# Sorting 800 tokens by group of experts in the last stage of a fused decoder kernel

## The reference, cut to what matters

```
x = rmsnorm(src + self_attention(src), norm1_w)        # 800 tokens x 256
shared = swiglu(x @ W_shared_in) @ W_shared_out        # 256 -> 2*512 -> 512 -> 256
g_probs = softmax(x @ Wg_gate + group_bias)            # 2 groups
g_idx = argmax(g_probs)
e_probs = softmax(x @ We_gate + expert_bias, over the 4 experts of group g_idx)
w = the two largest of e_probs * g_probs[g_idx], zero for the other 6 experts
h = swiglu(x @ W1_shared)                              # one hidden row for all experts
routed = sum over e of (h @ W2_experts[e]) * w[:, e]   # 8 experts, 512 -> 256
out = rmsnorm(x + shared + routed, norm2_w)
result = x_layer + tanh(g_ffn[1]) * out
```

## Time and profile before

| what | us |
|---|---|
| median of three runs | 582.63 (580.09 to 582.83) |
| the profiled execution, its own time | 584.23 |
| its span | 582.4 |
| TensorE busy in the span | 532.8 (91%) |
| VectorE, ScalarE, GpSimd busy | 282.0, 183.7, 125.6 |

### The profile page before, as it was taken

The page is one execution under the profiler, slowest core; times in us unless marked ns, Lnnn a source line. Parts: engine busy times, 40 slices in busy tenths (PEclk is TensorE's granted clock), DMA queues, the critical chain, the costliest instruction groups (busy, mean ns, idle before and its releaser), DMA issues. The chain is left out here.

```text
span 582.4 us, 9223 instructions
## 1 busy us (share of the span) xinstructions
PE 532.8 (91%) x3429; PEld 345.9 (59%) x3429; DVE 282.0 (48%) x660; ACT 183.7 (32%) x438; POOL 125.6 (22%) x146
## 2 busy tenths in 40 slices
PE   0989899899999879999999899999889999999995
PEld 0736575355556567788877677878535544544442
DVE  3436553121235575665676968887625222224242
ACT  1134331211103344555555545656532110000000
POOL 3112005001117252232232635341000000000000
PEclk9999968999999988999999999999989999999998
DMA  7989942279976697595573056000012000000000
GB/s 211 237 227 322 392 181 58 74 273 378 400 250 202 165 257 186 138 236 166 134 183 81 2 190 246 2 2 1 1 52 62 1 1 0 1 0 29 0 19 9
DMA packets 47087, 78.15 MB, mean 134 GB/s; under 512 B 6867, under 2 KB 36543, under 8 KB 46941
## 3 DMA queue, kind: packets, MB, share of 16 engines
q1 hardware_dynamic: 43841, 68.32, 38.0%
q0 software_dynamic: 3200, 9.22, 4.9%
HBM read 63.97 MB, written 12.13 MB: 131 GB/s over the span
## 5 line engine op out<-in xcount | busy, mean ns | idle before, releaser
L1392 PE MATMUL pb<-ring,big 128*128 128x512 f32 (+2 forms) x320 | 108.7, 593 | 2.3 <-DVE big L1343 1.2
L1392 PE MATMUL pb<-split 128*100 128x362 f32 (+2 forms) x320 | 78.3, 329 | 6.7 <-DVE nmx L1184 2.7
L1392 PEld LDWEIGHTS pb<-ring,big 128*128 128x128 f32 (+2 forms) x320 | 44.1, 166 | 59.4 <-issue 54.9
L1184 DVE TENSOR_REDUCE nmx<-pb 100x1 f32<-100x361 f32 x128 | 62.7, 527 | 25.6 <-PE pb L1392 25.2
L1392 PEld LDWEIGHTS pb<-split 128*100 128x100 f32 (+2 forms) x320 | 55.9, 183 | 16.7 <-issue 6.1
L860 ACT ACTIVATE big<-pb 121x400 f32<-121x400 f32 (+1 forms) x96 | 48.2, 505 | 23.9 <-PE pb L1392 21.6
L1364 DVE SCALAR_TENSOR_TENSOR ctxbuf<-pb,ctxbuf 128x256 f32<-128x256 f32 x48 | 23.2, 484 | 55.5 <-PE pb L1392 54.6
L1392 PE MATMUL pb<-big,arena 121*32 121x100 f32 (+3 forms) x1072 | 47.9, 264 | 1.5 <-ACT arena L710 1.2
L1392 PE MATMUL pb<-hT,ring 128*128 128x400 f32 x128 | 43.8, 501 | 0.5 <-DVE big L1343 0.5
L637 POOL TENSOR_TENSOR shift<-consts,nmx 100x400 fp32r<-100x400 f32 x32 | 28.3, 884 | 64.6 <-DVE nmx L1184 64.5
L1392 PE MATMUL pb<-hT,wgu 128*128 128x400 f32 (+2 forms) x108 | 39.7, 516 | 0.9 <-ACT hT L919 0.6
(11 more groups left out here) (242 smaller groups left out, 784.7 us busy)
## 6 DMA issues: line engine op xcount, KB each, us to landing
ring<-in_L_ffn_gate_up_proj SPq DMA_DIRECT2D x12, 1024.0 KB, 9.6
split<-kx_dram SPq DMA_DIRECT2D x64, 181.0 KB, 3.8
ring<-in_L_ffn_down_proj SPq DMA_DIRECT2D x12, 512.0 KB, 7.3
kx_dram<-split POOLq DMA_DIRECT2D x16, 362.0 KB, 4.9
ctxbuf<-in_L_ffn_gate_up_proj SPq DMA_DIRECT2D x4, 1024.0 KB, 9.6
ring<-in_L_ffn_W_experts SPq DMA_DIRECT2D x4, 1024.0 KB, 11.4
split<-qx_dram SPq DMA_DIRECT2D x64, 50.0 KB, 2.0
ctxbuf<-in_ctxT SPq DMA_DIRECT2D x6, 361.0 KB
```

The lines of the kernel that those rows point to most:

```text
L1184: nc.vector.tensor_reduce(nmx[:, t % 4, q:q + 1], PB[SB[n % 3]][0:T, 0:CTX], AX.X, ALU.max, negate=True) \
L1392: return nc.tensor.matmul(o, l, r, start=start, stop=stop)
```

## The change

Tokens are sorted by group into 928 slots: group 0 from slot 0 up, group 1 from slot 927 down, with 128 unused slots between. A tile is 116 slots, so no tile holds tokens of both groups, and each of the 8 tiles needs the down products of four experts alone. Which four is known only at run time: TensorE reads an offset for each tile into a register and addresses w2 with it.

- Logits are computed by batch, tokens on partitions. A product with a lower triangle and seven with ones give each token its position (as in layer 0), VectorE turns it into a slot.
- GpSimd scatters rows, token number and logits (267 numbers a row) of each batch to memory, then one scatter of 128 rows of zeros into the unused slots; SyncE loads them back by tiles, two tiles to a load of 116 partitions. Gates, transposes and the W1 units work on the sorted rows.
- Shared units and shared down products stay in token order. x + shared is added up by batch (e_base) and scattered to eb_dram, the rows of x to ex_dram; both get zeros in the unused slots first. Both come back by parts of two tiles (load_base, load_rest), some of them behind final products (e_down).
- The first half's shared units (0 to 3) stand among the last output products of attention; the first four batches are scaled (rms_rows) inside the attention loop, into free places of arena (stage).
- The result is stored by an indirect DMA of GpSimd for each tile, by token number; unused slots carry a number that is out of bounds.
- ScalarE takes exponentials of the gates between the silus of the shared and of the W1 units.

The diff, cut to its core:

```diff
-STARTS = [0, 128, 256, 768, 384, 512, 640]
-NF = len(STARTS)
-TAIL = STARTS.index(NT // 128 * 128)
-TAILN = NT % 128
-WHOLE = [c for c in range(NF) if c != TAIL]
-PARTS = [(0, 4), (4, 6), (6, 7)]
+ET = 116
+NS = NX * ET
+EX = D + 1 + 2 + NX
+FPARTS = [(0, 3), (3, 6), (6, 7), (7, 8)]
...
+            sp.wait_ge(s("b_scat"), 16 * (2 * NB + 1))
+            for g in range(NX // 2):
+                sp.dma_start(sorted_rows[0:ET, 2 * g:2 * g + 2, :],
+                             es_dram[2 * ET * g:2 * ET * (g + 1), :].rearrange("(i p) d -> p i d", p=ET)).then_inc(s(f"b_xg{g}"), 16)
+            sp.wait_ge(s("e_bst"), 16 * (NB + 1))
+            sp.wait_ge(s("n_tp"), NB // 2 * (turn("e") + 1) + NX // 2)
+            sp.wait_ge(s("e_gx"), 1)
+            def load_base(g):
+                sp.dma_start(hF[0:ET, 2 * g:2 * g + 2], eb_dram[2 * ET * g:2 * ET * (g + 1), :].rearrange("(i p) d -> p i d", p=ET)) \
+                    .then_inc(s(f"ld_F{g}"), 16)
+            def load_rest(g):
+                sp.dma_start(xF[0:ET, 2 * g:2 * g + 2], ex_dram[2 * ET * g:2 * ET * (g + 1), :].rearrange("(i p) d -> p i d", p=ET)) \
+                    .then_inc(s("ld_x"), 16)
+            load_base(0)
+            load_base(1)
+            sp.wait_ge(s("e_xst"), 16 * (NB + 1))
+            load_rest(0)
+            for g in range(1, NX // 2):
+                sp.wait_ge(s("e_down"), NB + 2 * g - 1)
+                load_rest(g)
+                if g >= 2:
+                    load_base(g)
+            sp.wait_ge(s("stored"), 16 * NX)
...
+            pool.wait_ge(s("n_hN"), NB * (turn("e") + 1))
+            pool.wait_ge(s("b_xs"), NB + 1)
+            pool.wait_ge(s("b_slot"), 3)
+            for b in range(NB):
+                nc.gpsimd.indirect_dma_start(es_dram, bass.IndirectOffsetOnAxis(slot[:, b:b + 1], 0), stage(b), None,
+                                             bounds_check=NS - 1, oob_is_err=False).then_inc(s("b_scat"), 16)
+            nc.gpsimd.indirect_dma_start(es_dram, bass.IndirectOffsetOnAxis(spare[:, 0:1], 0), zero_rows[:], None,
+                                         bounds_check=NS - 1, oob_is_err=False).then_inc(s("b_scat"), 16)
+            for d, name in ((eb_dram, "e_bst"), (ex_dram, "e_xst")):
+                nc.gpsimd.indirect_dma_start(d, bass.IndirectOffsetOnAxis(spare[:, 0:1], 0), zero_rows[:, 0:D], None,
+                                             bounds_check=NS - 1, oob_is_err=False).then_inc(s(name), 16)
+            for b in range(NB):
+                pool.wait_ge(s("e_base"), b + 1)
+                nc.gpsimd.indirect_dma_start(eb_dram, bass.IndirectOffsetOnAxis(slot[:, b:b + 1], 0), hN[:, b, :], None,
+                                             bounds_check=NS - 1, oob_is_err=False).then_inc(s("e_bst"), 16)
+            pool.wait_ge(s("c_res"), NB)
+            for b in range(NB):
+                nc.gpsimd.indirect_dma_start(ex_dram, bass.IndirectOffsetOnAxis(slot[:, b:b + 1], 0), x[:, b, :], None,
+                                             bounds_check=NS - 1, oob_is_err=False).then_inc(s("e_xst"), 16)
+            pool.wait_ge(s("b_tok"), 2)
+            for part, (a, z) in enumerate(FPARTS):
+                inverse_root("f", stdF, rstdF, only=part)
+                for i in range(a, z):
+                    pool.wait_ge(s("f_out"), i + 1)
+                    nc.gpsimd.indirect_dma_start(flat_out, bass.IndirectOffsetOnAxis(tok[0:ET, i:i + 1], 0), xF[0:ET, i, :], None,
+                                                 bounds_check=NT - 1, oob_is_err=False).then_inc(s("stored"), 16)
...
+            d_turned_copy(NB - 2)
+            d_sums_copy(NB - 1)
+            e_turned(0)
+            e_turned(1)
+            square(NB - 3)
+            shared_silu(0)
+            d_turned_copy(NB - 1)
+            square(NB - 2)
+            shared_silu(1)
+            square(NB - 1)
+            shared_silu(2)
+            e_turned(2)
+            shared_silu(3)
+            e_turned(3)
+            for u in range(4, 2 * FT):
+                shared_silu(u)
+            for g in range(NX // 2):
+                act.wait_ge(s("n_tp"), NB // 2 * (turn("e") + 1) + g + 1)
+                nc.scalar.activation(hTs[:, :, 2 * ET * g:2 * ET * (g + 1)], bank3(4 + g % 2, KT, 2 * ET), ACT.Copy) \
+                    .then_inc(s("n_hT"), 1)
+            act.wait_ge(s("e_gx"), 1)
+            nc.scalar.activation(ge, gl, ACT.Exp).then_inc(s("e_gexp"), 1)
...
+                if n == 28:
+                    rms_variance(0)
+                if n in (29, 30):
+                    rms_rows(0, range(2 * (n - 29), 2 * (n - 28)))
...
             rms_variance(1)
             rms_rows(1)
+            shared_hidden(0)
+            d_residual(NB - 1)
+            rms_variance(2)
+            shared_hidden(1)
+            rms_rows(2)
             link(nc.vector.tensor_scalar(growF, brow["n2"][:], tg[:, 3:4], None, ALU.mult))
+            shared_hidden(2)
+            shared_hidden(3)
...
+                dve.wait_ge(s(f"ld_F{i // 2}"), 16)
+                for p in range(2):
+                    v = 2 * i + p
+                    dve.wait_ge(s("e_down"), NB + v + 1)
+                    link(nc.vector.scalar_tensor_tensor(out=hF[0:ET, i, :], in0=PB[v % 8][0:ET, 0:D], scalar=we[:, i, 2 * p:2 * p + 1],
+                                                        in1=hF[0:ET, i, :], op0=ALU.mult, op1=ALU.add))
+                    nc.vector.scalar_tensor_tensor(out=hF[0:ET, i, :], in0=PB[v % 8][0:ET, D:2 * D], scalar=we[:, i, 2 * p + 1:2 * p + 2],
+                                                   in1=hF[0:ET, i, :], op0=ALU.mult, op1=ALU.add).then_inc(s("e_comb"), 1)
...
+            def shared_unit(u):
+                half, f = u // FT, u % FT
+                if u >= 2:
+                    pe.wait_ge(s("e_hid"), u - 1)
+                if u % FT == 0:
+                    pe.wait_ge(s("n_hT"), NB // 2 * turn("e") + 2 * (half + 1))
+                for w in range(2):
+                    for k in range(KT):
+                        last = mm(PB[S_BANKS[u % 2][w]][:, 0:HALF], wgu2[:, 0, k, F * w + 128 * f:F * w + 128 * f + 128],
+                                  hT[:, k, HALF * half:HALF * (half + 1)], k == 0, k == KT - 1)
+                last.then_inc(s("e_gu"), 1)
+            pe.wait_ge(s("d_max"), NG * NB)
+            ln_pe("e", range(0, 2), stage, E_TURN)
             d_to_tokens(NB - 1)
+            pe.wait_ge(s("ld_we"), 16 * 6)
+            pe.wait_ge(s("d_ptsb"), NG * NB)
+            shared_unit(0)
             bank6_part("Y", NB - 2, 0)
             d_turn_back(NB - 1)
+            shared_unit(1)
             bank6_part("Y", NB - 1, 0)
...
+            shared_unit(2)
+            ln_pe("e", range(2, 3), stage, E_TURN)
+            shared_unit(3)
+            pe.wait_ge(s("d_x2"), NB)
+            ln_pe("e", range(3, 4), stage, E_TURN)
+            for b in range(NB):
...
+                pe.wait_ge(s("n_hT"), NB // 2 * turn("e") + b // 2 + 1)
                 for k in range(KT):
...
+                    last = mm(PB[4][0:T, (2 + NX) * b:(2 + NX) * (b + 1)], hT[:, k, T * b:T * b + T], wge[:, k, :],
                               k == 0, k == KT - 1)
...
+            last.then_inc(s("lg"), 1)
+            shared_unit(4)
+            pe.wait_ge(s("b_oh"), 2)
+            mm(PB[5][0:T, 0:NB], consts[0:T, cs["lower"]], nflag, True, False)
+            for d in range(1, NB):
+                mm(PB[5][0:T, d:NB], ones[0:T, 0:T], nflag[:, 0:NB - d], False, d == NB - 1)
+            mm(PB[5][:, NB:NB + 1], ones[0:T, 0:128], nsum, True, True).then_inc(s("b_pos"), 1)
+            for u in range(5, 2 * FT):
+                shared_unit(u)
+            pe.wait_ge(s("b_slot"), 4)
+            for b in range(NB):
+                pe.wait_ge(s("e_hid"), FT if b < NB // 2 else 2 * FT)
+                for f in range(FT):
+                    last = mm(PB[shared_bank(b)][0:T, 0:D], hidS[:, f, T * b:T * b + T], wdn[:, f, :], f == 0, f == FT - 1)
+                last.then_inc(s("e_down"), 1)
...
+                pe.wait_ge(s(f"b_xg{g}"), 32)
+                if g < 2:
+                    pe.wait_ge(s("e_base"), g + 1)
+                else:
+                    pe.wait_ge(s("n_hT"), NB // 2 * (turn("e") + 1) + g - 1)
+                for k in range(KT):
+                    for q in range(2):
+                        at = (2 * k + q) * ET
+                        last = nc.tensor.transpose(PB[4 + g % 2][:, at:at + ET], sorted_rows[0:ET, 2 * g + q, 128 * k:128 * k + 128],
+                                                   ident[0:ET, 0:ET])
+                last.then_inc(s("n_tp"), 1)
...
+            for u in range(2 * FT, 4 * FT):
+                half, f = u // FT - 2, u % FT
+                if f == 0:
+                    pe.wait_ge(s("n_hT"), NB // 2 * (turn("e") + 1) + 2 * (half + 1))
+                if u < 2 * FT + 3:
+                    pe.wait_ge(s("e_base"), NB)
+                else:
```

(51 more changed lines are left out.)

240 lines of the change are left out of this document (87 added, 153 removed).

## The result

The changed kernel took 563.32 us, the median of four runs (558.8 to 565.35), beside 582.73 us (580.09 to 584.34) for the kernel before, measured beside it. The ratio is 0.9652 with a 95% interval of 0.9607 to 0.9696. That is 19.4 us less, where 24.3 were forecast (558.3 us, range 552.5 to 566.9). The profiled execution took 563.71 us, with a span of 561.8.

What follows compares the result with a forecast made beforehand. TensorE's matmul stream, busy 91% of the span, was taken as the bound. The stream ends 25.5 us earlier (32.0 - 6.5), the end is 1.2 longer: 24.3 us less, span 558.1, forecast 558.3 us, range 552.5 to 566.9.

Steps and rivals of the forecast that it cites:

- the clock: Rival, chance 0.20: thin logits and position products lower TensorE's clock for ten to fourteen us, giving 561.4 to 563.4 us.
- the units: Rival, chance 0.07: shared units don't fit beside attention's last batches, each waits behind ScalarE's work, giving 563.7 us.
- Steps 1 to 3: From the end of attention through logits, positions, shared units and eight shared down products; predicted to end at 463.1 us.
- step 3: Shared units 5 to 7, 8.1 us, and eight shared down products, 13.8 us; ends at 463.1.
- step 1: End of attention with four shared units interleaved, then logits 3.5 us and row scalings 1.0 us; ends at 436.5.
- Step 4: Nine scatters, then sorted rows loaded on about four DMA engines in 10.4 us; last load at 466.6, bounds 459.3 and 468.6.
- Step 5: Last transposes and copy end at 468.0; gates end about 475.5, covered by three second-product units and costed at nothing.
- Step 6: Eight units of 464 columns, 25.4 us plus 1.3 for a lowered clock, then 1.2 to the first down product; ends 495.9.
- Step 7: 128 final records, 54.9 us, ending at 550.8; register loads and register addresses for the operand costed at 0.
- slower rival: Chance 0.05: register addresses in the final products break TensorE's overlap, adding 45 us, to 603.
- Step 8: The end: 3.5 us of last small steps, scatter store landing in 2.8 us, 0.9 after it; ends at 558.1.
- GpSimd's queue: 27 scatters ahead of the final roots, 35 us, to 478; first root wanted after 515, so costed at nothing.

## Why the prediction was right, and where it was wrong

The direction, the mechanism and most of the size held: 64 fewer final records at an unchanged pace, and most of the wait at the end of attention filled. The time alone would not show it: 563.32 us lies nearer to two rivals (561.4 to 563.4 for the clock, 563.7 for the units) than to my 558.3, and it takes the trace to rule them out. In the order of its steps, with moments on the old clock:

- **Steps 1 to 3** were right, and 3.3 us too long by the end of step 3 (459.8, forecast 463.1). Nearly all of it is in step 1: four units and the logits were done at 433.5, forecast 436.5. The 3.5 us for the logits was 0.6 too much, since at full clock 32 records took 2.9. The other 2.4 lie before them. Of the 1.0 us for the row scalings inside attention VectorE's loop grew by 0.9, but TensorE reached its last products of the loop only 0.3 later (415.3, before 415.0); the rest is small work and waiting that took less room between the units, and I can't split it further. The rival of a clock that falls after the logits did not come: it was 1.00 in the windows at 427, 437 and 452. Nor did the units that don't fit beside the last batches: in the 11.5 us from 415.4 TensorE was busy for 11.2.
- **Step 4 failed in its size.** Scatters came every 1.30 us (forecast 1.29), and the loads were issued at 453.1 (forecast 455.2). A quarter of the engines was right, and so was 10.4 us for the data, as the run with the scatters held back shows: 0.27, 95 GB/s. What the trace of before could show only for 100 partitions (0.69), this case now shows for 116 (0.27 alone), for 112 and 4 (up to 1.00, scatters included) and for 58 (0.14 alone). The Trainium skill, DMA: Bandwidth & Descriptors, section Why a DMA increments its semaphore by 16 and not by 1, has a DMA run on the largest number of engines up to 16 that divides the slowest dimension of both sides; for 116, 112 and 58 partitions that works out to 4, 16 and 2. The runs agree with all three. By the same section of the Trainium skill a hardware queue takes the lowest-numbered engines, so that both halves of 58 would share the same two. The trace agrees: 2.2 engines and 43 GB/s, with the data of both halves. At that rate 0.99 MB take 23 us of the 28. The 10.4 us themselves were luck in part: the rows of before gave 12 to 12.4, less something for the overlap that I did not work out. What failed is the step from data to waiting: from the first issue to the last row I took 11.4 us, and it was 15.8. Some 2.5 are the scatters that run beside, which I had costed at nothing for the loads. The other 1.9 are the start and the last landing, there also without scatters (13.3 against 11.4). On the old clock the rows were in at 468.9 instead of 466.6, as the issue had come 2.1 earlier; the step's upper bound, 468.6, was passed.
- **Step 5** held, though the gates were finished at 478.7, forecast 475.5: the rows were later, and so was TensorE, which waited for none of them.
- **Step 6** held: 26.7 us for the eight units, forecast 25.4 + 1.3. The clock fell over the idle stretch as it had over thin ones before, and cost 1.2 us.
- **Step 7** held: 0.431 us a record, forecast 0.429, and the wait ahead of it was 1.41 us, forecast 1.2 (in step 6). The slower rival, with register addresses that break the overlap, is out.
- **Step 8 failed, with 3.8 of the 6.1 us by which the end came late:** 7.6 us from VectorE's last step to the end, forecast 3.8. I priced the store by the landing of layer 0's scatters, 2.8 us, and the 0.9 that followed a SyncE store. It starts 0.95 us after its releaser, lands 4.3 after its issue, and 2.3 us pass after that: 0.9 + 1.5 + 1.4 over what I took. Two mistakes lie in it. A landing of 100 rows was taken for one of 116, which step 4 had just found to be on few engines: the data moved for 2.0 us at 60 GB/s, against 1.1 at 94, and that is 0.9 of the 1.5. And the 0.9 us behind the last store was taken from another queue.

The account: -3.3 (steps 1 to 3), then +5.0 until the second product starts (469.7 against 468.0, so +1.7 in all), +0.6 from there to VectorE's last step, +3.8 for step 8: 6.1 us over the forecast span of 558.1. The 5.0 are 1.2 by which the loads started less early than TensorE came, 4.4 of waiting for their data, and 0.6 less for the last transposes. The median of the runs is nearer, 5.0 over. Part of that is luck: steps 1 to 3 were too long, and the loads, which TensorE then waits for, left 2.1 us early. Without it the median would have stood 7.1 over the forecast, at 565.4, still in the range.

Of GpSimd's queue, the part that was costed at nothing behind the loads is right: its last scatter of the 27 ended at 474.6, forecast 478, and no final root waited. What it had wrong is the loads beside it, 2.5 us.

What stays open: the 0.6 us that are left of the scatter's later landing, and what fills the 2.3 to 3.0 us after it on GpSimd's queue. That the interleaved units are worth 3 us rests on single profiles.

## What to carry to other kernels

Choose a tile's partitions for its DMAs as well as for its products: 116 keeps empty rows few, but loads over 112 and one over the 4 left gave back 7.5 to 8.1 us, two fifths of what the whole change had won. A split into equal parts can make it worse, so look at the divisors and not at the number of transfers. And look at every transfer of that tile: the store at the end moved on a quarter of the engines too, and nobody had priced it. When a store moves to another queue or becomes a scatter, price all three parts from rows of that queue: from the releaser to its start, from issue to landing, and from landing to the end of the program. At a program's end nothing hides them.
